# Routing from raw rows and one pipeline of 80 expert tiles: a change to the end of a conv-attention and mixture-of-experts block

## The chip, the cores and the metric

The kernel runs on one core of a Trainium2 chip. The metric is the device time of one execution in microseconds, as the median of a few runs. A profile of one execution comes with it; its time is given beside its span.

## The reference

The input is `x` of 8 x 32 x 32 x 192 in float32, that is 8192 tokens of 192 channels. Two attention layers with 12 heads come first; this case leaves both as they are. What matters here is the last part:

```python
x = x + conv_attention(group_norm(x))
t = tokens(x)
t = t + attention(layer_norm(t))          # the residual that routing starts from
t = t + experts(layer_norm(t))

def experts(t):                           # 16 experts, 192 -> 192 -> 192
    idx = argmax(t @ Wg.T + bg)           # one expert for each token
    for e in range(16):
        h = gelu(t @ W1[e].T + b1[e])
        out += (idx == e) * (h @ W2[e].T + b2[e])
```

The layer norm in front of the experts takes a mean and a variance over the 192 channels of each token, and has no weights: `(v - mean) / sqrt(var + 1e-5)`.

## The kernel before

The program is a row of stages, each a block of its own in which the five engines run their own lists of instructions and meet only at semaphores. Between two blocks all engines meet. The stages are: projections, attention with relative positions, projections, attention (`a2`), routing (`r`), experts (`e`). Only the last three matter here.

**Attention, `a2`.** It runs in 24 steps of 16 blocks, two steps to an iteration. SP's list holds stores of results, the rows of maxima that PE waits for at the start of a step, and work for later stages, held by the class `Early`: the residual rows (`early.tokens`, one DMA in each iteration but the first) and the experts' weights (`early.weights`).

**Routing, `route`.** 8192 tokens go in 4 rounds of 2048, a round being 16 tiles of 128 tokens (NT = 16). In a round:

- SP loads the attention outputs of the round in 6 DMAs (`load_attn`, L1178) into one of two buffers. `load_attn(0)` is the first thing in its list; the two small loads of the gate's weights and bias (L1182, L1183) follow, and `load_attn(1)`.
- DVE (`normalise`) adds them to the residual (L1307), takes the moments of each token (L1311, L1315), writes the mean behind the row (L1318), and hands variance + eps (L1319) to POOL, which raises it to -1/2 (`root`, L1219). DVE waits for that and writes normalised rows to a buffer of their own (L1323, 16 instructions).
- SP stores the residual rows with mean and root behind them to DRAM (`X3`, L1193); the experts read them from there.
- PE transposes the normalised rows (L1255), ACT copies them from PSUM (L1289), and PE multiplies them with the gate's weights (L1262, 64 passes of 16 columns).
- DVE (`choose`) adds the bias (L1336), finds the first largest logit (L1339 to L1344) and, with two products of PE (L1267, L1270, the ranks), the place of each token in its expert's list. Each step waits for the one before through the semaphore `ch`.
- POOL (`list_tokens`, L1224) writes the token numbers to their places with 16 scatters, each of 128 numbers of 4 bytes, to DRAM (`SLOTS`).

DVE's order is normalise(0), then for each round normalise(r + 1) and choose(r). PE's order is, for each round, transposes, logits, ranks. POOL issues the root of round r + 2 between the halves of the list of round r. After the last round DVE works out from the counts which expert each of 80 tiles belongs to and where its slots stand. POOL waits until all 64 scatters have landed and loads the slots (L1239).

**Experts, `experts`.** 80 tiles of 128 slots, in a hardware loop of two passes over 40 unrolled tiles (UN = 40). POOL gathers the rows of a tile from `X3` (L1476) into one of NB = 8 buffers and scatters results to the output (L1464). The scatter of tile k - LAG follows the gather of tile k, with LAG = NB - 2 = 6. DVE normalises (L1568); PE transposes (psX), applies layer one (psH), transposes again (psG) and applies layer two (psY), each one tile behind the other; ACT copies and applies gelu (L1536, L1548); DVE adds the residual (L1574). PE reads the tile's expert number from SBUF into a register. At the end of a pass POOL waits for all scatters; the next pass starts empty. POOL clears all gather buffers once before the first gather (L1458).

Of the kernel before, what the change touches and what calls it, by code (L numbers as in the profile page):

```python
# [42 lines left out]
def attention(nc, name, rel, scale, QK, RL, RLH, VN, OD, onehot_dram, early=None):  # L43
# [13 lines left out]
    with ExitStack() as ctx:  # L57
# [205 lines left out]
        def _(sp):  # L263
# [48 lines left out]
            def step(i, u, jobs, base, first, last):  # L312
# [770 lines left out]
def route(nc, name, XR, xl, X2DONE, ON, WG, BG, X3, SLOTS, TR, IXA):  # L1083
# [7 lines left out]
    with ExitStack() as ctx:  # L1091
# [9 lines left out]
        Os = [sb(f"attn{i}", [P, 2, NG, KT, GH * HD]) for i in range(2)]  # L1101
        XMs = [sb(f"xm{i}", [P, NT, C]) for i in range(2)]
        XT = sb("xmT", [CC, 2, PAIR])
# [5 lines left out]
        BGs = sb("bg", [P, E_N])  # L1109
        LG = sb("logits", [P, NT, E_N])  # L1110
# [31 lines left out]
        psL = ps("psL", [P, 512])  # L1142
# [6 lines left out]
        oload = [sem(f"oload{i}") for i in range(2)]  # L1149
# [14 lines left out]
        CH = 13 + NPRE  # L1164
        NM = 5
# [8 lines left out]
        def _(sp):  # L1174
# [6 lines left out]
            load_attn(0)  # L1181
# [16 lines left out]
        def _(pool):  # L1198
# [44 lines left out]
        def _(pe):  # L1243
            pe.wait_ge(made, NMADE)
            pe.wait_ge(wload, 32)
            for r in range(ROUNDS):
                XM = XMs[r % 2]
                pe.wait_ge(nm, r * NM + 5)
                for t in range(NT):
# [3 lines left out]
                    for c in range(2):  # L1253
                        at = 2 * P * (t % 2) + P * c
                        mm = nc.tensor.transpose(psT[0:CC, t // 2 % 4, at:at + P], XM[:, t, CC * c:CC * c + CC],  # L1255
                                                 ident[:, :])
                    if t % 2 == 1:
                        mm.then_inc(xtp, 1)
                pe.wait_ge(xts, r * (NT // 2) + NT // 2)
                for t in range(NT):  # L1260
                    for c in range(2):
                        mm = nc.tensor.matmul(psL[:, E_N * t:E_N * t + E_N], XT[:, c, P * t:P * t + P], WGs[:, c, :],  # L1262
                                              start=(c == 0), stop=(c == 1))
                mm.then_inc(lg, 1)

                pe.wait_ge(ch, r * CH + 6)
                nc.tensor.matmul(psK[:, 0:NT * E_N], TRI[:, :], OH[:, :, :].rearrange("p t e -> p (t e)"),  # L1267
                                 start=True, stop=False)
                pe.wait_ge(ch, r * CH + (8 + NPRE))
# [25 lines left out]
        def _(dve):  # L1295
            dve.wait_ge(wload, 32)
            dve.wait_ge(made, NMADE)
            dve.wait_ge(xl, X2DONE)
            nc.vector.tensor_copy(IDI[:, :], IDF[:, :]).then_inc(ids, 1)

            def normalise(r):
                X, XM, at = XR[:, tiles(r), :], XMs[r % 2], r * NM
# [14 lines left out]
                dve.wait_ge(nm, at + 2)  # L1317
                nc.vector.tensor_copy(X[:, :, C:C + 1], MV[:, :, 0:1]).then_inc(nm, 1)  # L1318
                nc.vector.tensor_scalar(VE[:, :, :], MV[:, :, 1:2], EPS, None, ALU.add).then_inc(nm, 1)  # L1319
                dve.wait_ge(nm, at + 4)  # L1320
# [4 lines left out]
                ins.then_inc(nm, 1)  # L1325

            def choose(r):
                n = [0]

                def link(ins):  # L1330
# [3 lines left out]

                dve.wait_ge(lg, r + 1)
                link(nc.vector.tensor_tensor(LG[:, :, :], psL[:, 0:NT * E_N].rearrange("p (t e) -> p t e", e=E_N),  # L1336
                                             BGs[:, :].rearrange("p (o e) -> p o e", o=1).to_broadcast([P, NT, E_N]),
                                             ALU.add))
# [60 lines left out]
def experts(nc, name, X3, W, wl, WDONE, TLs, IXA, OUT):  # L1399
# [4 lines left out]
    UN = 40  # L1404
    NB = 8
    LAG = NB - 2
    assert NTILE == 2 * UN and UN % NB == 0
    with ExitStack() as ctx:
# [42 lines left out]
        def _(pool):  # L1451
# [15 lines left out]
            with pool.Fori(0, NTILE // UN) as i:  # L1467
# [19 lines left out]
        def _(pe):  # L1487
# [15 lines left out]
            with pe.Fori(0, NTILE // UN) as i:  # L1503
# [25 lines left out]
        def _(act):  # L1529
# [8 lines left out]
            with act.Fori(0, NTILE // UN) as i:  # L1538
# [17 lines left out]
        def _(dve):  # L1556
# [4 lines left out]
            with dve.Fori(0, NTILE // UN) as i:  # L1561
# [16 lines left out]
class Early:  # L1578
# [6 lines left out]
    def __init__(self, nc, ctx, X2, weights):  # L1585
        self.X = ctx.enter_context(nc.sbuf_tensor("f_x", [P, T // P, CM], F32))
        self.W = [ctx.enter_context(nc.sbuf_tensor(f"f_w{i}", [CC + 1, 2, E_N, C], F32)) for i in (1, 2)]
        self.xl = ctx.enter_context(nc.semaphore("f_xl"))
        self.wl = ctx.enter_context(nc.semaphore("f_wl"))
# [14 lines left out]
def hybrid_block(nc, a, out):  # L1604
# [21 lines left out]
    with ExitStack() as ctx:  # L1626
# [4 lines left out]
        route(nc, "r", early.X, early.xl, early.XDONE, O2, a["wg"], a["bg"], X3, SLOTS, TR, IXA)  # L1631
# [53 lines left out]
```

## Time and profile before

| | us |
|---|---|
| median of 3 runs | 3399.32 |
| lowest and highest run | 3392.03, 3401.49 |
| the profiled execution | 3392.6 |
| its span | 3391.0 |
| mean granted TensorE clock | 0.896 of full speed |
| routing, from the block's start to the last wait for scatters | 2926 to 3108 |
| experts, from the first gather to the end | 3119 to 3391 |

The difference between the profiled time and the span lies ahead of the first and behind the last recorded instruction. In the rows below a line of the timeline gives the start and the duration in microseconds, the engine, the line of the kernel, the operation, what it writes and reads, the count, and in square brackets how long the engine had been idle before it and what ended that. A row of the groups gives busy time and mean ns of one instruction, then the idle time before these instructions and what ended it. A row of the windows gives the stretch, its length, for PE, PEld (weight loads), DVE, ACT and POOL the busy time and the count, and then the granted clock as a share of full speed, the busy share of the DMA engines, and GB/s.

### The profile page before, as it was taken

What the parts mean: (1) busy time and instruction counts of PE and PEld (TensorE: products, weight loads), DVE (VectorE), ACT (ScalarE), POOL (GpSimd) and SP (SyncE); (2) the same over time, 40 slices, a digit from 0 to 9 for tenths busy, and PEclk for the clock granted to TensorE, in tenths of its full rate; (3) what the DMA queues carried; (4) which work ended last, traced back from release to release, by engine and by line L of the source; (5) the groups of instructions that cost most, each with busy time, mean ns of one, the idle gap of its engine ahead of it and who ended that gap; (6) DMA issues with size and microseconds to landing.
All of it is one profiled execution on the core that took longest, in us unless ns stands there. A gap on an engine that the chain in (4) does not pass through costs nothing. (4 is left out here: it accounts for less than half of the span.)

```text
span 3391.0 us, 64293 instructions
## 1 busy us (share of the span) xinstructions
PE 2932.4 (86%) x17814; PEld 1145.2 (34%) x17815; DVE 2457.8 (72%) x4481; ACT 1852.6 (55%) x2382; POOL 1034.4 (31%) x1685
## 2 busy tenths in 40 slices
PE   4887699999999999996995999999999999662877
PEld 2665122222222222224652222222222222261666
DVE  3553698998899998943645999999999999351211
ACT  1343066776666666672331577777777777410332
POOL 0000333333333333313222223333333332154655
PEclk9777599999999999997986899999999999865777
DMA  4766555444554445524655432222222222360211
GB/s 80 206 199 196 116 105 105 103 100 96 100 109 101 95 98 101 108 54 115 179 165 118 90 89 74 74 74 72 74 73 74 75 72 59 114 54 11 58 50 34
DMA packets 234003, 327.80 MB, mean 97 GB/s; under 512 B 63820, under 2 KB 162966, under 8 KB 229298
## 3 DMA queue, kind: packets, MB, share of 16 engines
q0 software_dynamic: 76576, 192.17, 25.7%
q1 hardware_dynamic: 157332, 134.44, 15.5%
q8 instruction: 51, 0.84, 0.1%
q14 instruction: 44, 0.36, 0.1%
HBM read 217.71 MB, written 109.19 MB: 96 GB/s over the span
## 5 line engine op out<-in xcount | busy, mean ns | idle before, releaser
L499 DVE TENSOR_REDUCE a_halfmax<-a_psR 128x1 f32<-128x512 f32 x3072 | 1964.0, 685 | 193.0 <-PE a_psR L350 174.7
L454 ACT ACTIVATE a_probs<-a_psS 128x1024 f32<-128x1024 f32 x1536 | 1488.4, 1021 | 795.2 <-PE a_psS L368 790.8
L368 PE MATMUL a_psS<-a_qrows,a_krows 121*128 121x512 f16 (+1 forms) x3072 | 807.7, 385 | 53.6 <-DMA a_qrows<-relh 49.2
L379 PE MATMUL a_psO<-a_probs,a_v 128*32 128x512 f32 x6144 | 827.9, 611 | 1.2 <-ACT a_probs L454 1.2
L350 PE MATMUL a_psR<-a_kmax,a_qmax 64*128 64x512 f16 x3072 | 685.4, 400 | 80.2 <-DMA a_qmax<-relh 43.3
L350 PEld LDWEIGHTS a_psR<-a_kmax,a_qmax 64*128 64x128 f16 x3072 | 161.1, 93 | 1072.2 <-DVE a_halfmax L499 951.5
L368 PEld LDWEIGHTS a_psS<-a_qrows,a_krows 121*128 121x128 f16 (+1 forms) x3072 | 243.2, 98 | 427.9 <-issue 163.1
L204 POOL DMA_DIRECT2D a_qmax<-qk x240 | 122.4, 510 | 666.8 <-PE a_psO L379 601.6
L188 POOL DMA_DIRECT2D a_qrows<-qk x240 | 123.6, 515 | 276.6 <-PE a_psO L379 257.2
L830 PE MATMUL p_psQ<-p_xnT,p_wqk 96*128 96x512 f32 x384 | 190.3, 660 | 20.4 <-DVE p_xnT L987 13.9
L379 PEld LDWEIGHTS a_psO<-a_probs,a_v 128*32 128x32 f32 x6144 | 121.4, 108 | 184.2 <-issue 175.9
L1574 DVE TENSOR_TENSOR e_y<-e_psY,e_x 128x192 f32<-128x192 f32 x80 | 28.6, 357 | 173.8 <-PE e_psY L1499 103.5
L1021 DVE SCALAR_TENSOR_TENSOR p_half<-p_qk,p_sc,p_half 128x2048 f16<-128x2048 f32 (+1 forms) x36 | 72.8, 2031 | 110.8 <-ACT p_half L925 110.8
L918 ACT ACTIVATE p_qk<-p_psQ,p_bqk 128x512 f32<-128x512 f32 x96 | 65.6, 686 | 144.3 <-PE p_psQ L830 144.3
L205 POOL DMA_DIRECT2D a_kmax<-qk x240 | 121.9, 508 | 15.8
L830 PEld LDWEIGHTS p_psQ<-p_xnT,p_wqk 96*128 96x128 f32 x384 | 80.2, 213 | 126.5 <-issue 111.9
L193 POOL DMA_DIRECT2D a_qrows<-rel x96 | 48.4, 504 | 209.7 <-PE a_psO L379 208.3
L200 POOL DMA_DIRECT2D a_v<-v x96 | 53.5, 557 | 190.8 <-PE a_psO L379 190.1
L873 PE MATMUL p_psR<-p_half,p_relThalf 64*128 64x64 f16 x1920 | 97.5, 239 | 14.8 <-DVE p_rel L1059 12.7
L933 ACT CAST p_rel<-p_psR 128x256 f16<-128x256 f32 x192 | 57.2, 391 | 92.2 <-PE p_psR L873 92.2
L1499 PE MATMUL e_psH<-f_w,e_xmT 96*128 (+1 forms) x320 | 89.8, 415 | 16.1 <-ACT e_xmT L1536 9.5
L1464 POOL DMA_INDIRECT out<-e_y,e_slots x80 | 81.0, 1013 | 73.9 <-DVE e_y L1574 49.5
(162 smaller groups left out, 2310.8 us busy)
## 6 DMA issues: line engine op xcount, KB each, us to landing
a_qrows<-qk POOLq DMA_DIRECT2D x240, 128.0 KB, 4.0
qk<-p_half SPq DMA_DIRECT2D x96, 256.0 KB, 3.4
v<-p_v SPq DMA_DIRECT2D x48, 512.0 KB, 6.2
a_qrows<-rel POOLq DMA_DIRECT2D x96, 256.0 KB, 4.6
a_v<-v POOLq DMA_DIRECT2D x96, 256.0 KB, 3.1
a_krows<-qk POOLq DMA_DIRECT2D x168, 128.0 KB, 3.8
a_qmax<-qk POOLq DMA_DIRECT2D x288, 64.0 KB, 2.3
a_kmax<-qk POOLq DMA_DIRECT2D x240, 64.0 KB, 2.3
```

The lines of the kernel that those rows point to most:

```text
L188: pool.dma_start(A[buf][c][at, :, :], qk(s, TERMS[n][0], 0)).then_inc(loaded[buf], 16)
L204: pool.dma_start(AM[buf][0][of, :, :], qk_pair(s, TERMS[n][0], 0, r)).then_inc(loadedm[buf], 16)
L205: pool.dma_start(KM[buf][of, :, :], qk_pair(s, TERMS[n][1], 1, r)).then_inc(loadedm[buf], 16)
L350: mm = nc.tensor.matmul(psR[:, slot, :], AM[b][half][at, p, P * qt:P * qt + P], KM[b][at, p, 512 * half:512 * half + 512], start=True, sto ...
L368: mm = nc.tensor.matmul(psS[:, (2 * n + j) % 4, :], K[buf][:, h, keys], A[buf][kt % NA][:, h, queries], start=True, stop=True)
L379: mm = nc.tensor.matmul(psO[32 * h:32 * h + 32, :], V[buf][:, kt, h, :], PT[:, blk % 2, h, :], start=(kt == 0), stop=(kt == KT - 1))
L454: nc.scalar.activation(PT[:, blk % 2, 2 * pair:2 * pair + 2, :], psS[:, b0:b0 + 2, :], ACT.Exp, scale=scale).then_inc(exped, 1)
L499: nc.vector.tensor_reduce(mx[:, unit, half:half + 1], psR[:, slot, :], AX.X, ALU.max)\
L830: mm = nc.tensor.matmul(psQ[:, n % 2, :], WQK[:, c, P * m:P * m + P], XN[:, c, 512 * q:512 * q + 512], start=(c == 0), stop=(c == 1))
L873: mm = nc.tensor.matmul(o[:, :, x, :], table.rearrange("p k h -> p (k h)"), q[:, :, xx, :] if hw == 0 else q[:, :, :, xx], start=(i == 0), ...
L1464: pool.indirect_dma_start(OUT, bass.IndirectOffsetOnAxis(ap=IX[:, k:k + 1], axis=0), Y[:, q, :], None, bounds_check=T - 1, oob_is_err=Fals ...
L1499: mm = nc.tensor.matmul(dst[:, 0:C], xT[0:k, c, :], w[0:k, c, bass.ds(e, 1), :] .rearrange("p o n -> p (o n)"), start=(c == 0), stop=(c == 1))
```

## The change

In attention's last iteration SP loads the attention outputs of routing's first round, one DMA a block, in six blocks, after it has waited that the earlier steps' stores are done. In routing PE works on the raw residual rows instead of normalised ones. By `(x - m) r W = r (x W - m sum(W))` the mean and the root are applied to the 16 logits: DVE multiplies the mean with the column sums of the gate's weights (two small products of PE), subtracts, multiplies with the root, and adds the bias. Normalised rows are no longer written. PE's logits run one round ahead of its ranks, with a second PSUM bank; DVE's moments run two rounds ahead of its choice, and POOL's roots three ahead. The experts become one unrolled pipeline of 80 tiles with ten buffers, the scatter eight tiles behind the gather.

```diff
@@ attention, SP
+                    if early is not None and last and u == 0 and blk == 6:
+                        for qh in range(QH):
+                            sp.wait_ge(stored[qh], 16 + 16 * 2 * NG)
+                    if early is not None and last and u == 0 and blk in range(6, 12):
+                        sp.wait_ge(pvdone, s * PVS + blk + 2)
+                        early.attn(sp, OD, blk - 6)
@@ class Early
+        self.O = ctx.enter_context(nc.sbuf_tensor("f_attn", [P, 2, NG, KT, GH * HD], F32))
+    def attn(self, sp, OD, n):
+        sp.dma_start(self.O[:, n // NG, n % NG, :, :], OD[n]).then_inc(self.ol, 16)
@@ route, SP
-            load_attn(0)
             sp.dma_start(WGs[:], ...)
@@ route, POOL
             root(0)
             root(1)
+            root(2)
...
-                if r + 2 < ROUNDS:
-                    root(r + 2)
+                if r + 3 < ROUNDS:
+                    root(r + 3)
@@ route, PE
-                pe.wait_ge(nm, r * NM + 5)
+            for c in range(2):
+                mm = nc.tensor.matmul(psC[:, 0:E_N], ONE[0:CC, :], WGs[:, c, :], start=(c == 0), stop=(c == 1))
+            mm.then_inc(wsum, 1)
+            def logits(r):
+                pe.wait_ge(x3, r + 1)
...
+            logits(0)
+            for r in range(ROUNDS):
+                if r + 1 < ROUNDS:
+                    logits(r + 1)
+                ranks(r)
@@ route, DVE
-            dve.wait_ge(wload, 32)
...
-                dve.wait_ge(rsq, r + 1)
-                for t in range(NT):
-                    ins = nc.vector.tensor_scalar(XM[:, t, :], X[:, t, 0:C], X[:, t, C:C + 1], X[:, t, C + 1:C + 2],
-                                                  ALU.subtract, ALU.mult)
...
+                link(nc.vector.tensor_tensor(MS[:, :, :], X[:, :, C:C + 1].to_broadcast(wide),
+                                             WS[:, :].rearrange("p (o e) -> p o e", o=1).to_broadcast(wide), ALU.mult))
                 dve.wait_ge(lg, r + 1)
+                link(nc.vector.tensor_tensor(LG[:, :, :], psL[:, r % 2, 0:NT * E_N]..., MS[:, :, :], ALU.subtract))
+                dve.wait_ge(rsq, r + 1)
+                link(nc.vector.tensor_tensor(LG[:, :, :], LG[:, :, :], X[:, :, C + 1:C + 2].to_broadcast(wide), ALU.mult))
+                link(nc.vector.tensor_tensor(LG[:, :, :], LG[:, :, :], BGs[:, :]..., ALU.add))
...
             normalise(0)
+            dve.wait_ge(wload, 32)
+            dve.wait_ge(wsum, 1)
+            nc.vector.tensor_copy(WS[:, :], psC[:, 0:E_N]).then_inc(wsum, 1)
+            normalise(1)
+            dve.wait_ge(wsum, 2)
             for r in range(ROUNDS):
-                if r + 1 < ROUNDS:
-                    normalise(r + 1)
+                if r + 2 < ROUNDS:
+                    normalise(r + 2)
                 choose(r)
@@ experts
-    UN = 40
-    NB = 8
+    UN = NTILE
+    NB = 10
     LAG = NB - 2
...
-            with pool.Fori(0, NTILE // UN) as i:
+            for i in range(1):
```

## Rows read from the trace of the kernel before

**Rows 1.** The page, busy time and share of the span by engine

```profile
PE 2932.4 (86%) x17814; PEld 1145.2 (34%) x17815; DVE 2457.8 (72%) x4481; ACT 1852.6 (55%) x2382; POOL 1034.4 (31%) x1685
```

**Rows 2.** Timeline of routing, single instructions

```profile
2930.26 1.01 POOL L1214 MEMSET r_empty<- 128x1104 int32 x1
...
2935.45 0.20 DVE L1299 CAST r_tokenIdsInt<-r_tokenIds 128x64 int32<-128x64 f32 x1 [9.70 <-DMA r_bg<-in_bg]
...
2977.82 0.17 DVE L1359 CAST r_placeOfInt<-r_placeOf 128x16 int32<-128x16 f32 x1
...
2978.89 1.87 POOL L1224 DMA_INDIRECT slots<-r_tokenIdsInt,r_placeOfInt  x1 [14.09 <-DVE r_placeOfInt L1359]
...
3041.62 11.03 PE L1262 MATMUL r_psL<-r_wg,r_xmT 96*128 96x16 f32 x63 [1.28 <-ACT r_xmT L1289]
...
3060.50 0.42 DVE L1336 TENSOR_TENSOR r_logits<-r_psL,r_bg 128x256 f32<-128x256 f32 x1 [23.24 <-remote]
...
3068.93 0.95 POOL L1224 DMA_INDIRECT slots<-r_tokenIdsInt,r_placeOfInt  x1 [11.49 <-DVE r_placeOfInt L1359]
...
3087.85 0.96 POOL L1224 DMA_INDIRECT slots<-r_tokenIdsInt,r_placeOfInt  x1 [0.30 <-issue]
...
3107.64 0.94 POOL L1239 DMA_INDIRECT r_slotsOfTile<-slots,r_slotRow  x1 [18.83 <-DMA slots<-r_tokenIdsInt,r_placeOfInt]
...
3110.72 0.22 DVE L1394 CAST r_slotsOfTileF<-r_slotsOfTile 80x128 f32<-80x128 int32 x1 [37.22 <-DMA r_slotsOfTile<-slots,r_slotRow]
```

**Rows 3.** Groups by line in routing, 2926 to 3112 us

```profile
L1224 POOL DMA_INDIRECT slots<-r_tokenIdsInt,r_placeOfInt x64 | 64.5, 1008 | 53.5 <-DVE r_placeOfInt L1359 35.5 <-issue 18.0
...
L1262 PE MATMUL r_psL<-r_wg,r_xmT 96*128 96x16 f32 x256 | 42.5, 316 | 8.4 <-ACT r_xmT L1289 4.7 <-issue 3.5
...
L1255 PE MATMUL r_psT<-r_ident,r_xm 128*96 128x128 f32 x128 | 20.9, 341 | 27.8 <-DVE r_xm L1323 27.8
...
L1323 DVE TENSOR_SCALAR r_xm<-f_x 128x192 f32<-128x192 f32 x64 | 19.9, 389 | 16.3 <-POOL f_x L1219 16.3
...
L1311 DVE BATCH_NORM_STATS2 r_stats<-f_x 128x6 f32<-128x192 f32 x64 | 17.0, 345 | 0.1
...
L1307 DVE TENSOR_TENSOR f_x<-f_x,r_attn 128x1536 f32<-128x1536 f32 x8 | 13.7, 1754 | 0.1
...
L1315 DVE BATCH_NORM_AGGREGATE r_meanvar<-r_stats 128x2 f32<-128x6 f32 x64 | 4.7, 151 | 0.1
...
L1219 POOL TENSOR_TENSOR f_x<-r_variance,r_half 128x16 f32<-128x16 f32 x4 | 11.8, 2944 | 27.7 <-DVE r_variance L1319 27.7
```

**Rows 4.** Windows of two stretches, the wait for scatters and the experts

```profile
3076.00:3116.00 40.00, 0.40 (x1) 0.18 (x1) 0.47 (x2) 0.00 (x0) 12.22 (x16) 0.50 0.01 1
...
3254.00:3300.00 46.00, 36.27 (x174) 30.51 (x174) 10.07 (x30) 17.30 (x47) 27.15 (x27) 0.79 0.20 55
```

**Rows 5.** Groups by line in the experts, 3110 to 3391 us

```profile
L1499 PE MATMUL e_psH<-f_w,e_xmT 96*128 (+1 forms) x320 | 89.8, 415 | 16.1 <-ACT e_xmT L1536 9.5 <-issue 6.0 <-ACT e_h L1548 0.6
...
L1464 POOL DMA_INDIRECT out<-e_y,e_slots x80 | 81.0, 1013 | 73.9 <-DVE e_y L1574 49.5 <-issue 19.3 <-DMA out<-e_y,e_slots 5.1
...
L1493 PE MATMUL e_psX<-e_ident,e_xm 128*96 128x128 f32 x160 | 39.3, 336 | 32.3 <-DVE e_xm L1568 30.1 <-issue 2.1
...
L1458 POOL MEMSET e_x<- 128x1552 f32 x1 | 1.4, 1396 | 0.1
```

**Rows 6.** Timeline of POOL in the experts: scatters of tiles 4, 30, 43, 47, 73

```profile
3145.34 1.02 POOL L1464 DMA_INDIRECT out<-e_y,e_slots  x1 [2.49 <-DVE e_y L1574]
...
3227.38 1.02 POOL L1464 DMA_INDIRECT out<-e_y,e_slots  x1 [2.50 <-DVE e_y L1574]
...
3274.89 1.02 POOL L1464 DMA_INDIRECT out<-e_y,e_slots  x1 [2.20 <-DVE e_y L1574]
...
3287.66 1.02 POOL L1464 DMA_INDIRECT out<-e_y,e_slots  x1 [2.51 <-DVE e_y L1574]
...
3371.82 1.02 POOL L1464 DMA_INDIRECT out<-e_y,e_slots  x1 [2.04 <-DVE e_y L1574]
```

More of the change, by code:

```diff
@@ L1080, with route @@
 EMPTY = 1 << 20
[L1083 removed]
+def route(nc, name, early, ON, WG, BG, X3, SLOTS, TR, IXA):
     NT = PAIR // P
@@ L1099, in sem @@
             return ctx.enter_context(nc.semaphore(f"{name}_{n}"))
-        Os = [sb(f"attn{i}", [P, 2, NG, KT, GH * HD]) for i in range(2)]
-        XMs = [sb(f"xm{i}", [P, NT, C]) for i in range(2)]
-        XT = sb("xmT", [CC, 2, PAIR])
+        XR = early.X
+        Os = [early.O, sb("attn", [P, 2, NG, KT, GH * HD])]
+        XT = sb("xT", [CC, 2, PAIR])
         ST = sb("stats", [P, NT, 6])
@@ L1109, in route @@
         BGs = sb("bg", [P, E_N])
+        WS = sb("wgSums", [P, E_N])
+        MS = sb("meanPart", [P, NT, E_N])
         LG = sb("logits", [P, NT, E_N])
@@ L1141, in route @@
         psT = ps("psT", [P, 4, 512])
-        psL = ps("psL", [P, 512])
+        psL = ps("psL", [P, 2, 512])
         psK = ps("psK", [P, 512])
@@ L1148, in route @@
         filled = sem("filled")
-        oload = [sem(f"oload{i}") for i in range(2)]
+        oload = [early.ol, sem("oload")]
+        wsum = sem("wsum")
         x3 = sem("x3")
@@ L1163, in route @@
         NPRE = NT.bit_length() - 1
-        CH = 13 + NPRE
-        NM = 5
+        CH = 16 + NPRE
+        NM = 4
         NMADE = 12
@@ L1245, in _ @@
             pe.wait_ge(wload, 32)
-            for r in range(ROUNDS):
-                XM = XMs[r % 2]
-                pe.wait_ge(nm, r * NM + 5)
+            for c in range(2):
[3 more added lines that the diff above has]
+                pe.wait_ge(x3, r + 1)
                 for t in range(NT):
@@ L1259, in _, with ranks @@
                 pe.wait_ge(xts, r * (NT // 2) + NT // 2)
+                if r >= 2:
+                    pe.wait_ge(ch, (r - 2) * CH + 2)
                 for t in range(NT):
                     for c in range(2):
-                        mm = nc.tensor.matmul(psL[:, E_N * t:E_N * t + E_N], XT[:, c, P * t:P * t + P], WGs[:, c, :],
+                        mm = nc.tensor.matmul(psL[:, r % 2, E_N * t:E_N * t + E_N], XT[:, c, P * t:P * t + P], WGs[:, c, :],
                                               start=(c == 0), stop=(c == 1))
                 mm.then_inc(lg, 1)
-                pe.wait_ge(ch, r * CH + 6)
+            def ranks(r):
+                pe.wait_ge(ch, r * CH + 9)
                 nc.tensor.matmul(psK[:, 0:NT * E_N], TRI[:, :], OH[:, :, :].rearrange("p t e -> p (t e)"),
                                  start=True, stop=False)
-                pe.wait_ge(ch, r * CH + (8 + NPRE))
+                pe.wait_ge(ch, r * CH + (11 + NPRE))
                 nc.tensor.matmul(psK[:, 0:NT * E_N], ONE[:, :], PRE[NPRE % 2][:, :, :].rearrange("p t e -> p (t e)"),
                                  start=False, stop=True).then_inc(rk, 1)
+            logits(0)
[3 more added lines that the diff above has]
+                ranks(r)
             pe.wait_ge(ch, ROUNDS * CH)
@@ L1295, in _ @@
         def _(dve):
-            dve.wait_ge(wload, 32)
             dve.wait_ge(made, NMADE)
-            dve.wait_ge(xl, X2DONE)
+            dve.wait_ge(early.xl, early.XDONE)
             nc.vector.tensor_copy(IDI[:, :], IDF[:, :]).then_inc(ids, 1)
             def normalise(r):
-                X, XM, at = XR[:, tiles(r), :], XMs[r % 2], r * NM
+                X, at = XR[:, tiles(r), :], r * NM
                 dve.wait_ge(oload[r % 2], r // 2 * 96 + 96)
@@ L1399, in experts @@
 def experts(nc, name, X3, W, wl, WDONE, TLs, IXA, OUT):
-    UN = 40
-    NB = 8
+    UN = NTILE
+    NB = 10
     LAG = NB - 2
-    assert NTILE == 2 * UN and UN % NB == 0
+    assert UN % NB == 0
     with ExitStack() as ctx:
@@ L1501, in layer @@
                 mm.then_inc(done, 1)
-            with pe.Fori(0, NTILE // UN) as i:
+            for i in range(1):
                 ex = [None] * UN
@@ L1536, in to_sbuf @@
                 nc.scalar.copy(dst[0:CC], src[0:CC, 0:2 * P].rearrange("p (c t) -> p c t", c=2)).then_inc(done, 1)
-            with act.Fori(0, NTILE // UN) as i:
+            for i in range(1):
                 n = i * UN
@@ L1560, in _ @@
             nc.vector.sem_inc(ys, 2)
-            with dve.Fori(0, NTILE // UN) as i:
+            for i in range(1):
                 n = i * UN
@@ L1587, in __init__ @@
         self.W = [ctx.enter_context(nc.sbuf_tensor(f"f_w{i}", [CC + 1, 2, E_N, C], F32)) for i in (1, 2)]
+        self.O = ctx.enter_context(nc.sbuf_tensor("f_attn", [P, 2, NG, KT, GH * HD], F32))
         self.xl = ctx.enter_context(nc.semaphore("f_xl"))
+        self.ol = ctx.enter_context(nc.semaphore("f_ol"))
         self.wl = ctx.enter_context(nc.semaphore("f_wl"))
```

17 lines of the change are left out of this document (10 added, 7 removed).

## The prediction

> **What bounds the kernel now.** The page comes first. PE is busy for 86% of the span [rows 1], but the change touches only the end: the routing of tokens to experts (from about 2926 us) and the expert layers (3118 to 3391 us). Of attention it touches only what SP issues in the last steps. So I went on to the windows by stage, the groups by line, and the instructions in order of time, of these 465 us.
>
> In routing no engine is the bound for long. DVE starts only when two small loads have landed, 9.70 us after it was free [rows 2]. From then on the four rounds are a chain: DVE adds and takes moments, POOL takes the root, DVE normalises (64 instructions, 19.9 us, after 16.3 us of waiting for POOL), PE transposes and multiplies, DVE chooses [rows 3]. The last round shows the cost: DVE sits idle for 23.24 us before it can read the logits at 3060.50 [rows 2]. POOL's 64 scatters of token numbers take 64.5 us, with 0.3 us between two, and wait 35.5 us for places [rows 3]. But POOL is not the last word: its last 16 scatters are issued from 3068.93 on, the last one at 3087.85, and it then waits 18.83 us, until 3107.64, until they have landed [rows 2]. In those 40 us nothing else is busy, and the DMA share is 0.01 [rows 4]. I read that as scatters that land more slowly than they are issued. That share can't show where writes are pending; the wait can.
>
> In the experts PE looks like the bound (four groups of matmuls: psH 89.8, psX 39.3 us, and two like them [rows 5]), but at a granted clock of 0.79 [rows 4], so between its levels of 1.2 and 2.4 GHz, which it falls between when it waits. POOL issues a gather and a scatter for each tile: 2 x (1.01 + 0.30) = 2.64 us. Its scatters 4 and 30 start 82.0 us apart, 43 and 73 start 96.9 us apart [rows 6]: 3.16 and 3.23 us a tile. The pattern repeats every 12.8 us (3274.89, 3287.66): four tiles are 10.6 us of issue and about 2.2 us of waiting for a result [rows 6].
>
> **Routing, the issuing side.** (a) The first attention outputs are loaded during attention's last steps, and the two small loads go first and are awaited only after the first moments. DVE can start when POOL's constants stand, at 2930.26 + 1.01 = 2931.3, instead of 2935.45 [rows 2]: 4.2 us. The six loads that move onto SP in attention are about 0.4 us of queue time each, behind waits for values that PE has long been past; behind them in the queue stands only the store of the half step, whose data is not read until its own load. I cost this at nothing; if the row of maxima after them came late, PE would wait, at most some 3 us, once.
> (b) The normalisation goes: 19.9 us of DVE and the 16.3 us in front of it. Three operations on 256 elements a round (scaled mean, times root, plus bias) come in, 0.42 us each by the operation that reads the logits now [rows 2] and 0.04 between them: 1.4 us a round. One round before the choice is now (13.7 + 17.0 + 4.7)/4 = 8.9, with the two small copies 9.3 us [rows 3].
> (c) DVE does three of these before its first choice: 2931.5 + 27.9 + 0.2 = 2959.6. PE starts its first round at about 2935 and needs (20.9 + 42.5)/4 = 15.9, with the turn through ACT 17 us a round [rows 3]. It does two rounds before the first ranks: 2969. The ranks' second product and the four last operations add about 4 us, and POOL starts 0.9 us later, as before (2977.82 + 0.17 to 2978.89 [rows 2]): 2974 against 2978.9, so 4.9 us earlier. Here the round ahead costs something: without it the first list would start at about 2970.
> (d) After that POOL is the slowest of the issuing side: 16 x 1.31 = 21 us a round against 17 + 2.4 for PE and 9.3 + 9.2 for DVE (20 steps of at most 0.46), and one root of 2.9 us among them [rows 3]. Its last scatter would be out at 2974 + 84 + 3 = 3061, before at 3087.85 + 0.96 = 3088.8 [rows 2]: 28 us earlier.
>
> **Routing, the landing side.** The slots can be read only when all 64 have landed. No row gives a scatter's landing, so its price is bounded. I take 3 us for the first to land, as the load of the slots behind them took (3107.64 to 3110.72 [rows 2]). All 64 then took 3107.6 - 2981.9 = 125.7 us, or 1.96 us each, with gaps and with two of the stores of the residual between them. The last 16 alone took 3107.6 - 3071.9 = 35.7 us, or 2.23 us each [rows 2]. Both are more than the 1.31 us of an issue. If the landing rate is what counts, an earlier issue only lengthens the queue. At 1.96 the end moves by what the start moves: -4.9 us (3102.7). At 2.23 it is 2977 + 142.7 = 3119.7: +12 us. I take 1.96, because the changed stage too has stores among its scatters; 2.23 stays in the range. The other end is a landing that keeps up with the issue: 3061 plus the 18.8 us tail of before, -28 us, or at the most 3061 + 3, -44 us. PE's logits of the last round took 18.9 us (3041.62 to 3060.50 [rows 2]) where the mean is 10.6 [rows 3]; if all rounds are so slow, PE sets 27 us a round and the last list starts some 14 us later than POOL alone would have it, still before the landing at 3102.7.
>
> The Trainium skill ("DMA: Bandwidth & Descriptors", Anatomy of one DMA) says that a DMA has about 2 us of fixed cost, mostly the receipt of the write, after which the semaphore fires. By that rule alone every scatter would be in 2 us after its issue: the first rival at its far end. The wait of 18.83 us behind the last issue [rows 2] speaks against it. The same page (Specifications) says that writes below 512 B are done as a read and a write; the scatters write 4 B each, and this agrees with a rate below that of the issue.
>
> **Experts.** (e) One pipeline of 80 in place of two of 40. Scatters 30 and 43 are 3274.9 - 3227.4 = 47.5 us apart; at 3.2 us a tile it would be 41.6 [rows 6]. So the drain and refill cost 5.9 us, and they go.
> (f) Ten buffers, and a scatter that follows its gather by eight tiles. If POOL's wait goes away, a tile costs 2.64: -0.56 x 70 = -39 us. If it stays, nothing. PE's weight: its matmul groups fill most of the stage, it waited only 32.3 us before psX, much of that at the two starts [rows 5], and a POOL that has scattered all finished tiles must wait whatever its buffers. More buffers let PE find a fifth tile in a period now and then: (10.6 + 2.2)/4 = 3.2 becomes 13.2 + 2.2 over 5 = 3.08. I take -0.1 x 70 = -7 us, near the end at zero, because the wait of 2.2 us is for results, not for buffers.
> (g) The clearing of the gather buffers grows by a quarter (1.4 us [rows 5]) on the way to the first gather: +0.4. Constants in place of register sums shorten queues that the rows show as hidden: nothing. If code for the second 40 tiles has to be fetched and that were late, it would cost some us; the first 40 had the same need and ran at 3.16, no slower than the second.
>
> **Sum**: -4.9 - 5.9 - 7 + 0.4 = -17.4. The profiled execution took 3392.6 us (span 3391.0), which is 6.7 below the median of the three runs. 3392.6 - 17.4 = 3375.2, and beside the median 3382.
>
> **Rivals.**
> - The landing keeps up with the issue: -28 instead of -4.9, total -40, 3359 (-56 and 3343 if it trails by 3 us alone). For it: the stores that shared the DMA engines are earlier too. Against: 2.23 us each for the last 16, with nothing beside them. The Trainium skill's fixed cost (above) would have it so. 0.17.
> - Ten buffers free POOL: 2.64 us a tile, total -49, 3350. For it: 49.5 us of POOL's waits were for results [rows 5], some of which start from late gathers. Against: PE's own groups. A fuller PE would also keep its clock. 0.13.
> - Nothing but the drain goes, and landing costs 2.23: +12.2 - 5.9 + 0.4 = +6.7 at no gain a tile, -0.3 with it; 3399 to 3406, no change that can be told. 0.22.
> - The other side: with scatters queued without a break the landing gets slower, not only longer. It decides from 64 x (R - 1.96) = 17.4 + 10, R = 2.39 us; at 2.5 it is +17, 3416. For it: 2.23 beats 1.96 where less else ran. 0.18.
> - My forecast: 0.30, between 3374 and 3390.
>
> The bound of a change that can be told is 0.3% or 10 us here. Faster: the first two, the forecast: 0.60; same 0.22; slower 0.18. Both signs hold chances, so 8 in 10 need 3350 (the second rival) to 3410 (between +6.7 and +17); the forecast's own range is 3370 to 3392.
>
> **What would show it.** POOL's first scatter at about 2974 and its last before 3065; then a wait of some 40 us for landing until about 3103, against 18 before: that is the step I lean on. If the wait is under 25 us and ends before 3085, the first rival holds; beyond 3125, the fourth. DVE's long wait for the last logits is gone. In the experts no gap in the middle, and 3.1 us a tile; at 2.7 the second rival holds. PE's clock there stays near 0.8. The prediction is wrong at its root if the landing time isn't a rate per scatter.

## The result and the profile after

The changed kernel takes 3358.48 us (median of 4, 3352.58 to 3363.97) beside 3395.68 us for the kernel before (4 runs, 3388.42 to 3401.49): a ratio of 0.9888, 95% interval 0.9865 to 0.9911, or 38 us less (30 to 46). I had forecast 17.4 us less, 3375 to 3382 us. The time lies in the wide range (3350 to 3410), which was drawn to take in rivals on both sides, but below the forecast's own (3370 to 3392); the gain is more than twice what I summed.

The profiled execution spans 3350.9 us, 40.1 less than before's. The first thing to read is where the touched stages begin. Timeline, attention's last output, of before and then of the changed kernel:

```profile
2925.33 0.42 DVE L519 TENSOR_TENSOR a_out<-a_psR,a_recip 128x256 f32<-128x256 f32 x1
```

```profile
2909.25 0.42 DVE L525 TENSOR_TENSOR a_out<-a_psR,a_recip 128x256 f32<-128x256 f32 x1
```

16.1 of the 40.1 us had been gained by then, in stages whose code is the same but for six late loads. All of it is there before the second attention begins (its first loads: 1831.8 and 1815.7 us). So from here on I count from attention's last output; the experiments show that this offset is chance. Behind it stand 465.7 us before and 441.7 after: 24.0 less, 16.6 of them up to the first gather (193.6 and 177.0), 7.4 behind it (272.0 and 264.7).

Timeline of routing in the changed kernel, the rows that answer to [rows 2]:

```profile
2915.25 0.20 DVE L1319 CAST r_tokenIdsInt<-r_tokenIds 128x64 int32<-128x64 f32 x1 [5.58 <-POOL r_empty L1222]
...
2957.14 0.42 DVE L1378 TENSOR_TENSOR r_place<-r_psK,r_expertBase 128x256 f32<-128x256 f32 x1 [7.53 <-PE r_psK L1285]
...
2959.60 1.86 POOL L1232 DMA_INDIRECT slots<-r_tokenIdsInt,r_placeOfInt  x1 [13.60 <-DVE r_placeOfInt L1382]
...
2963.44 10.15 PE L1276 MATMUL r_psL<-r_wg,r_xT 96*128 96x16 f32 x64 [1.06 <-ACT r_xT L1310]
...
2989.01 0.60 PE L1276 MATMUL r_psL<-r_wg,r_xT 96*128 96x16 f32 x2 [1.02 <-issue]
...
2998.18 0.19 PE L1276 MATMUL r_psL<-r_wg,r_xT 96*128 96x16 f32 x1 [2.61 <-issue]
...
3013.46 0.42 DVE L1378 TENSOR_TENSOR r_place<-r_psK,r_expertBase 128x256 f32<-128x256 f32 x1 [28.85 <-PE r_psK L1285]
...
3015.28 1.02 POOL L1232 DMA_INDIRECT slots<-r_tokenIdsInt,r_placeOfInt  x1 [10.78 <-DVE r_placeOfInt L1382]
...
3054.70 0.96 POOL L1232 DMA_INDIRECT slots<-r_tokenIdsInt,r_placeOfInt  x1 [0.30 <-issue]
...
3074.78 0.95 POOL L1248 DMA_INDIRECT r_slotsOfTile<-slots,r_slotRow  x1 [19.12 <-DMA slots<-r_tokenIdsInt,r_placeOfInt]
```

Read it from the end. The wait for landing is 19.12 us, as long as before's 18.83 [rows 2], although the last 32 scatters now follow each other without a break; my forecast needed some 40 us here. So the slots are read when the issuing side is done plus 19 us. The issuing side in turn has one hole, 10.78 us, and the rows above it say whose: DVE waits 28.85 us for ranks that stand in PE's queue behind the last round's logits, and after the first 36 of them those come one or two at a time, mostly with 0.5 to 2.6 us of "issue" ahead of each. The round before, at 2963.44, was not held up, though POOL had been issuing scatters since 2959.60. Windows over these stretches (busy us and instructions of PE, PEld, DVE, ACT, POOL; granted clock, DMA share, GB/s) show PE all but empty in the second stretch while POOL issues, and at the lower of its levels (0.50, 1.2 GHz):

```profile
2975.00:2987.00 12.00, 10.34 (x69) 9.66 (x69) 7.75 (x24) 4.84 (x16) 9.09 (x10) 0.78 1.17 81
2987.00:3009.00 22.00, 4.34 (x21) 5.07 (x20) 0.00 (x0) 0.00 (x0) 13.40 (x14) 0.50 0.47 28
...
3150.00:3200.00 50.00, 38.75 (x191) 33.97 (x190) 9.65 (x30) 14.63 (x45) 31.59 (x31) 0.81 0.20 56
```

Groups by line in the experts, changed kernel (against [rows 5]): matmuls (psH 88.0 us) and scatters as before, and POOL's waits for results 40.6 us where they were 49.5.

```profile
L1492 POOL DMA_INDIRECT out<-e_y,e_slots x80 | 81.3, 1016 | 66.8 <-DVE e_y L1602 40.6 <-issue 21.8 <-DMA out<-e_y,e_slots 4.3
```

### The profile page after: what moved, and what is told of

It reads as the page before. It is cut to its first block and busy times, and to the rows that moved or that the text cites. A ratio compares the mean times of both kernels' runs of the same rounds, so it can differ in the third digit from the quotient of the medians.

```text
span 3350.9 us, 63879 instructions
## 1 busy us (share of the span) xinstructions
PE 2924.0 (87%) x17818; PEld 1147.6 (34%) x17818; DVE 2438.7 (73%) x4430; ACT 1849.2 (55%) x2379; POOL 1037.2 (31%) x1684
## 5 line engine op out<-in xcount | busy, mean ns | idle before, releaser
L836 PE MATMUL p_psQ<-p_xnT,p_wqk 96*128 96x512 f32 x384 | 188.5, 654 | 19.3 <-DVE p_xnT L993 13.9
L1564 ACT COPY e_xmT<-e_psX 96x256 f32<-96x256 f32 x80 | 29.5, 369 | 196.9 <-PE e_psX L1521 179.1
L1492 POOL DMA_INDIRECT out<-e_y,e_slots x80 | 81.3, 1016 | 66.8 <-DVE e_y L1602 40.6
```

Source lines behind the costliest of these rows:

```text
L836: mm = nc.tensor.matmul(psQ[:, n % 2, :], WQK[:, c, P * m:P * m + P], XN[:, c, 512 * q:512 * q + 512], start=(c == 0), stop=(c == 1))
L1492: pool.indirect_dma_start(OUT, bass.IndirectOffsetOnAxis(ap=IX[:, k:k + 1], axis=0), Y[:, q, :], None, bounds_check=T - 1, oob_is_err=Fals ...
```

## The experiments

One table first, worked out from each kernel's timeline: attention's last output (us from the span's start), and from there POOL's first scatter, the end of its last, the load of the slots, the first gather; then first gather to end, and the time between results 35 and 45 of the experts.

```
kernel                    attention  first  last   slots  gather  to end  35-45
before                      2925.3   53.6  163.5  182.3  193.6   272.0   40.4
changed                     2909.3   50.4  146.4  165.5  177.0   264.7   30.0
e1 route only               2913.0   47.8  140.4  158.5  169.8   274.2   39.1
e2 experts only             2909.6   56.9  179.8  199.0  210.5   258.6   31.2
e3 eight buffers            2924.3   50.4  143.8  161.8  173.0   262.3   30.5
e4 no round ahead           2924.0   44.0  159.2  176.7  188.2   261.1   32.6
e5 no scatters of results   2922.4   50.4  141.4  157.3  168.8   163.0   17.5
e6 56 scatters              2920.7   47.9  130.8  142.2  153.0   261.4   30.6
e7 22 scatters              2917.4   47.8  114.4  130.2  139.1   259.8   30.4
e8 known expert             2914.0   50.4  144.2  159.9  171.3   253.6   27.0
e9 results nowhere          2929.3   47.8  143.3  159.4  171.0   265.5   33.9
e10 gathers nowhere         2928.5   50.3  143.8  160.0  171.7   266.1   29.6
e11 late loads              2913.0   51.2  159.6  175.1  186.6   262.4   30.7
e12 set up early            2912.9   50.4  143.0  159.8  167.3   263.5   31.3
```

The first column runs from 2909.3 to 2929.3 with no tie to the kernel: before, e2 and e11, which have no early loads, have 2925.3, 2909.6 and 2913.0; e3, e9 and e10, which have them, 2924.3 to 2929.3. So the 16.1 us of the first comparison are no effect of the change that these profiles show.

A second thing varies between profiles, in routing. Take, in each kernel, the time from a round's first transpose on PE to its last logit. In twelve of the fourteen kernels one round is held up, while all others take 16.8 to 19.7 us: 35.9 us in the changed kernel, 40.6 in e2, 31.8 in e4 (its third round), 20.7 in e5, 48.3 in e11, 30.9 to 35.0 in the other seven. Before's slowest took 19.4 and e7's 17.3. So before's 193.6 us to the first gather were a good draw: e2, with the same routing, has 210.5.

**e1 and e2: the change in two halves.** e1 has the changed routing and loads with before's experts, e2 the reverse.

```diff
-    UN = NTILE
-    NB = 10
+    UN = 40
+    NB = 8
```

> The changed routing and early loads with the experts of before (two turns of 40 tiles, eight buffers). In the profiled execution of the changed kernel the stretch from attention's last output to the first gather is 177.0 us, before it is 193.6: 16.6 us less. Theory A (the gain of the whole change is what the touched stages show, 16.6 in routing and 7.4 in the experts): this kernel gains about 17 us on the kernel before, ratio 0.995, its first gather comes about 177 us after attention's last output, and first gather to end is about 272 us, as before. Rival (the other 16 us, which the profile shows in stages whose code is the same, belong to the change, by way of the early loads or where things lie in memory): it gains 30 us or more, and its attention ends about 16 us earlier than before's. Rival of the prediction (the experts gain more than they show alone): under 10 us.

> The kernel before with the experts alone changed: one run of 80 tiles, ten buffers. Theory A: first gather to end is about 265 us instead of 272, the gain is 7 us, ratio 0.998, all of it the drain in the middle. Prediction's step (f), 0.1 us a tile from the buffers: 12 to 13 us, ratio 0.996. Rival (changed stages shift others by where code and data lie): more than 15 us, with attention's end moved.

e1: 0.9931 (0.9907 to 0.9955), 23 us (15 to 32) less. e2: 0.9959 (0.9941 to 0.9977), 14 us (8 to 20) less. Together 37, the whole, so nothing suggests that the halves touch each other. e1's interval allows theory A's 17 us and just reaches the rival's 30; e1's attention did end 12.3 us earlier than before's, but e2's, without the early loads, ended 15.7 us earlier. In e2, POOL stood 27.15 us before its last list, where before's stood 11.49 [rows 2].

**e3: eight buffers.**

```diff
-    NB = 10
+    NB = 8
```

> The changed kernel with eight buffers instead of ten, still one run of 80 tiles. Theory A (what a tile costs does not hang on buffers): the time of the changed kernel within 2 us, 3.2 us a tile, about 37 us under the kernel before. Rival (the ten buffers do give 0.1 us a tile and something else takes it back): 7 us slower than the changed kernel, 3.3 us a tile.

0.9905 (0.9880 to 0.9930), which overlaps the changed kernel's interval; the time alone doesn't exclude 7 us. The tiles do: results 5 to 35 and 45 to 75 come every 3.16 us (mean of both) with eight buffers, every 3.15 with ten (changed, e2, e4, e11: 3.10 to 3.21). A gain of 0.1 us a tile from the last two buffers is not there; one of a few hundredths couldn't be told with one profile of e3.

**e4: no round ahead.**

```diff
-            logits(0)
             for r in range(ROUNDS):
-                if r + 1 < ROUNDS:
-                    logits(r + 1)
+                logits(r)
                 ranks(r)
```

> The changed kernel, but PE makes the ranks of a round before the logits of the next one (no round ahead). In the changed kernel DVE waits 7.53 us for the first ranks behind the second round's logits, and POOL's first scatter is 50.4 us after attention's last output. Theory A: the first scatter comes 7 to 8 us earlier, POOL is the slowest of the issuing side, and the last scatter is out 5 to 8 us earlier, so 5 to 8 us under the changed kernel. Rival (PE's logits of the last rounds are what POOL waits for, 10.78 us in the changed kernel, and without the round ahead each such slow round is paid in full): the last scatter is out 5 to 15 us later, and the kernel is slower by as much.

0.9947 (0.9929 to 0.9964), 14 us worse than e3 on the same chip. Both expectations were half right: the first scatter is 6 us earlier than in the changed kernel and e3 (44.0 against 50.4; 4 us against the kernels with 47.8), but POOL then waits 18.36 and 12.29 us for the third and fourth list, and the last scatter is out 13 to 19 us later. The round ahead costs at the start and pays at the end.

**e6 and e7: fewer scatters of token numbers.** e6 leaves out the last 8, e7 all but the first of each half list in the first three rounds. The slots not written stay empty, so some rows aren't gathered. Each has one run, its profile.

```diff
-                list_tokens(r, NT // 2, NT)
+                if r < ROUNDS - 1:
+                    list_tokens(r, NT // 2, NT)
```

```diff
-                for t in range(t0, t1):
+                for t in range(t0, t1 if r == ROUNDS - 1 else t0 + 1):
```

> The changed kernel; left out are the last 8 of the 64 scatters of token numbers, so that the list of the last 1024 tokens stays empty. POOL's wait for landing behind its last issue was 17.5 to 19.3 us in six profiles. Theory R (a rate: about 2.2 us a scatter at the end, 1.26 to issue): the wait gets shorter by 8 x (2.2 - 1.26) = 8 us, to about 11, and the slots are read 18 us earlier. Theory D (a delay: a scatter takes some 19 us to land however many are behind it): the wait stays at 18 to 19 us, the slots are read 10 us earlier.

> The changed kernel; left out are 14 of the 16 scatters of each of the first three rounds, so that 6 are issued there and the 16 of the last round follow alone. Theory A (PE's logits of round 3, 25 to 30 us where an undisturbed round takes 10, are held up by the scatters in flight): they take 10 to 13 us, and PE's waits for its own issue between them (9.5 to 16.9 us) are gone. Rival (the stores of the residual hold them up): they stay above 18 us. For landing, theory R (rate): the last 16 need 3 + 16 x 2.2 = 38 us from the first issue, a wait of 18 us behind the last; theory Q (a backlog of all 64): under 8 us; theory D (delay): 18 to 19 us.

POOL's load of the slots in e6, and in e7:

```profile
3062.95 0.95 POOL L1249 DMA_INDIRECT r_slotsOfTile<-slots,r_slotRow  x1 [11.39 <-DMA slots<-r_tokenIdsInt,r_placeOfInt]
```

```profile
3047.58 0.95 POOL L1248 DMA_INDIRECT r_slotsOfTile<-slots,r_slotRow  x1 [15.86 <-DMA slots<-r_tokenIdsInt,r_placeOfInt]
```

With 8 fewer the wait falls to 11.39 us, as theory R had it; a fixed delay of 19 us is out. e7, with the last 16 alone, waits 15.86, near theory R's 18 and not under 8: the first three rounds leave hardly any backlog. Yet a single rate would leave a longer wait behind 24 scatters without a break (e6) than behind 16 (e7), and it was shorter. Over an unbroken run, less 3 us for the first, a scatter lands in 1.6 us (e6, 24 of them), 1.65 to 1.77 (32 of them, the nine kernels with the changed order) or 2.05 to 2.26 (16 of them: before, e2, e4, e7). The wait depends on how many went last, but one number a scatter doesn't give it; what else sets it is open.

e7 answers the second question too. Its logits of the last round on PE's timeline:

```profile
2987.84 10.56 PE L1276 MATMUL r_psL<-r_wg,r_xT 96*128 96x16 f32 x64 [1.17 <-ACT r_xT L1310]
```

All 64 run on in 10.56 us; in the changed kernel the same 64 take 29.5 us (2981.95 to 3011.5), and in the others with all scatters and this order 13.7 (e5) to 26.6. The stores of the residual run in both, so they alone don't hold PE up; the scatters are needed. They are not enough: the round before took 10.15 us beside them, and e4's last round 10.1. In the changed kernel the last residual store was issued at 2973.89, just ahead of the round that is held up; scatters without stores weren't tried.

**e5, e9, e10: which part of POOL's work the experts feel.** e5 leaves out the scatters of results for tiles 0 to 69, and with them the gathers' waits for those scatters. e9 issues those with row numbers out of bounds, so that nothing is written; e10 does that to all gathers and writes all results, computed from zeros. The diffs are e5's, and the one of e9 and e10.

```diff
+                if k >= UN - NB:
                     pool.indirect_dma_start(OUT, bass.IndirectOffsetOnAxis(ap=IX[:, k:k + 1], axis=0), Y[:, q, :], None,
```

```diff
-  bass.IndirectOffsetOnAxis(ap=IX[:, k:k + 1], axis=0)
+  bass.IndirectOffsetOnAxis(ap=NO[:, 0:1], axis=0)
```

> The changed kernel; left out are the scatters of the experts' results for tiles 0 to 69 (only the last ten are written), so POOL issues one indirect DMA a tile, a gather, instead of two: 1.31 us instead of 2.62. A tile costs 3.10 to 3.19 us in the kernels with one run of 80 tiles. Theory A (POOL's two issues and the waits round them set the tile, as in the prediction's terms): the tile falls to PE's own work, about 2.5 us (36.27 us of 46 in a window of before, at a granted clock of 0.79, rows 4, x 3.2), the kernel gains 40 us or more on the changed one. Theory B (PE's matmuls and the way they are released set it, whatever POOL does): 3.1 us, no change beyond 5 us. Theory C (PE's results come late while POOL issues, so the lateness goes with the issues but part of the chain stays): in between, 2.7 to 2.9 us.

> The changed kernel; the scatters of results of tiles 0 to 69 are issued as before, but with row numbers out of bounds, so POOL spends its 1.3 us on each and nothing is written (those rows of the output stay unwritten). Without those issues a tile costs 1.78 us, with them and their writes 3.10 to 3.19. Theory I (the time of POOL's issues, 2 x 1.31 = 2.62 us, is the bound, and the rest is how PE meets it): 2.6 to 2.75 us a tile, about 30 us less than the changed kernel. Theory W (the writes that the scatters set off hold PE's results or POOL's waits back): under 2.6 us is impossible by the issues, so 2.62 with PE at its high clock as well; the two differ in the next run. Theory P (PE's results come late whenever POOL issues two a tile, written or not): 3.1 us, no change.

> The changed kernel; the scatters of results are real, but all gathers have row numbers out of bounds, so POOL spends the same time on them and nothing is read (PE works on zeros, the output is wrong). Theory P (what two issues a tile do to PE, whatever moves): 3.1 us a tile. Theory W (the scatters' writes are what delays): 3.0 to 3.1 us a tile here too, but 2.6 where the scatters go nowhere. Theory G (the landing of gathers, some 9 us ahead of their use, sets the pace): 2.6 to 2.75 us here.

e5: 0.9614 (0.9595 to 0.9632), some 93 us under the changed kernel, 1.78 us a tile, below even theory A. e9: 0.9906 (0.9877 to 0.9934); e10: 0.9900 (0.9880 to 0.9919): no gain, 3.14 and 3.22 us a tile. Windows of the same stretch, e5, then e9:

```profile
3150.00:3200.00 50.00, 50.00 (x345) 47.88 (x344) 18.37 (x57) 27.49 (x87) 28.10 (x30) 1.00 0.19 50
```

```profile
3150.00:3200.00 50.00, 40.00 (x188) 34.85 (x186) 9.40 (x29) 14.51 (x44) 32.69 (x32) 0.76 0.11 28
```

With one issue a tile PE is never idle and runs at its upper level (1.00, 2.4 GHz). With two, though the DMA share falls from 0.20 to 0.11, it is back between its levels. The 50 us hide that it is at one level or the other. Two neighbouring stretches of e9:

```profile
3187.90:3194.70 6.80, 5.84 (x20) 5.01 (x21) 1.85 (x6) 2.38 (x8) 4.24 (x5) 0.50 0.08 20
3194.70:3201.50 6.80, 4.17 (x28) 3.54 (x27) 1.29 (x4) 2.06 (x7) 3.93 (x4) 1.00 0.17 43
```

In the changed kernel, between its 6th and 79th gather, PE spends 109 us at the lower level, 92% busy, with 3.1 matmuls started a us, and 123 us at the upper, 71% busy, with 4.3; in e5 at the upper level it starts 6.8. A tile has 12 matmuls. By an estimate from these numbers a tile takes 3.9 us at the lower level, 2.8 at the upper, and 1.75 where PE is never short of work. So at the lower level PE, nearly full, can't keep up with POOL's 2.62 us; at the upper it can, and its busy share is near 1.78/2.62 = 0.68.

The timeline of e5 and of e9 shows the two rhythms:

```profile
3201.63 1.00 POOL L1503 DMA_INDIRECT e_x<-x,e_slots  x1 [0.75 <-issue]
```

```profile
3198.52 1.03 POOL L1507 DMA_INDIRECT e_x<-x,e_slots  x1 [0.30 <-issue]
3199.30 0.33 ACT L1579 ACTIVATE e_h<-e_psH 128x192 f32<-128x192 f32 x1 [3.11 <-PE e_psH L1530]
3199.69 0.42 PE L1524 MATMUL e_psG<-e_ident,e_h 128*96 128x128 f32 x2 [1.50 <-issue]
3200.81 0.36 DVE L1605 TENSOR_TENSOR e_y<-e_psY,e_x 128x192 f32<-128x192 f32 x1 [4.56 <-remote]
...
3202.08 1.02 POOL L1495 DMA_INDIRECT out<-e_y,e_nowhere  x1 [2.54 <-DVE e_y L1605]
```

POOL issues back to back (0.30 between two) until it has no result left. Meanwhile psH, whose matmuls are recorded at 3197.38 to 3198.19, is read only at 3199.30; the result of the tile is late in turn, and POOL waits 2.54 us for it, whether it writes that result or not. Theory P's number holds against those of W and G: with two issues a tile it stays at 3.1 to 3.2 us whatever moves, and 2.62 of it is the issues themselves. What makes up the rest isn't settled. The clock is a rival that the expectations didn't name: POOL's pace leaves PE idle, the lower level follows, and there PE is slower than POOL.

**e8: no reading of the expert.**

```diff
-                        ex[m] = pe.value_load(TLs[0:1, bass.ds(n + m, 1)], min_val=0, max_val=E_N - 1)
+                        ex[m] = m // (UN // E_N)
```

> The changed kernel; PE takes the expert of a tile as a constant (tile number / 5) instead of reading it from the routing's list, so results of most tiles are computed with another expert's weights, and the read and the register sums of addresses go. Theory A (PE's instruction stream, its loads and address sums, is what makes its results late): the tile falls below 3.0 us, 10 us or more in all. Theory B (they are hidden): 3.1 us, no change beyond 3 us.

The profile has 253.6 us to the end and 3.06 us a tile, the fastest of those with all issues, but the ratio is 0.9884 (0.9863 to 0.9905), the changed kernel's. Undecided: a gain over the changed kernel is not shown.

**e11: the loads back in routing.**

```diff
+            load_attn(0)
             sp.dma_start(WGs[:], WG.rearrange("(c p) n -> p c n", p=CC)).then_inc(wload, 16)
```

> The changed kernel, but the first round's attention outputs are loaded in the routing block again, ahead of the two small loads (part (a) of the change undone). In the changed kernel DVE starts its additions 6.1 us after attention's last output, before 10.2 us. By the prediction's step (a): DVE starts 4.2 us later, and the first scatter comes 4 us later, at 52 to 54 us behind attention's last output where six runs had 47.8 or 50.4. Rival (PE or POOL have slack that takes it up): DVE's start moves, the first scatter does not.

DVE's additions start 9.9 us behind attention instead of 6.1, the first scatter at 51.2 where others had 47.8 or 50.4. So the start moves by step (a)'s 4 us and the first scatter by 1 to 3. The third list then came 24 us behind the second: PE's transposes of the last round, begun at 2980.1, were still followed by a wait of 19.17 us ahead of its logits at 3014.5. Whether the loads did that or chance, one profile can't say.

**e12: POOL's setting up inside the wait.** From its trace of the changed kernel: after the slots are read, POOL clears and copies for 5 us before the first gather. Here it does so while the last scatters land.

```diff
             pool.wait_ge(scat, ROUNDS * 16 * NT)
```
(ahead of this line now stand the identity, the rows of ones and the clearing of `e_x`; the gathers read `f_slotsAll` itself)

> The changed kernel; what POOL does at the start of the experts' block (identity, rows of ones, clearing of ten gather buffers: 3.7 us to the first gather's list, in the changed kernel's trace 3081.34 to 3084.99) is done in the routing block, in POOL's wait for the last scatters to land (15.5 to 19.3 us in eleven profiles), and the slots are used where they stand instead of being copied (1.26 us). Theory A (that wait is dead time for POOL): from the slots' load to the first gather 11.1 to 11.6 us become 6.5 us, 5 us less in all, with the landing wait shorter by what POOL does in it and the slots read as early as before. Rival (landing goes on more slowly while POOL works, or other engines' block change takes the time anyway): the first gather comes less than 2 us earlier. The time goes to about 33 + 5 us under the kernel before, ratio 0.989.

Slots' load to first gather: 7.5 us, in the changed kernel 11.5. The slots are read no later (159.8 us; 157.3 to 165.5 in the others with this routing, but for e11). That is 4 of the 5 us. The time, 3355.79 us and 0.9899 (0.9878 to 0.9921), can't be told from the changed kernel's. Of the kernels that compute everything, none is shown to be faster than the changed one.

## Why the prediction was right or wrong

**(a) Right.** DVE starts 6.0 us behind attention's last output, 10.1 before: 4.1, forecast 4.2. What reaches the first scatter is less (e11).

**(b), (c) Right.** A round before the choice takes 9.1 us (9.3 forecast); the four operations on the logits take 0.42 each. The first scatter moved by 3.2 us (4.9 forecast), and its price for the round ahead is there as I said: 7.53 us of DVE waiting, and 4 to 6 us in e4 where I had said 4.

**(d), issuing side: the bound failed, and the size in part.** I had POOL as the slowest, at 21 us a round, and DVE's long wait for logits gone. PE's last round took 35.9 us instead of 17 (2975.5 to 3011.5), DVE waited 28.85 us for the ranks behind it, and POOL 10.78 before the third list. Forecast 28 us earlier than before; measured 17.1, and 19 to 23 in seven more profiles of this routing (all but e11's), against before's one good draw. By place the forecast was nearer: 135.7 us behind attention's last output, measured 140.4 to 146.4. I had seen one slow round in before (18.9 us from its first logit to DVE's reading, 13.1 of them recorded matmuls) and priced it as harmless because landing would be later anyway; landing wasn't.

**(d), landing: this step failed, and it is the bulk of the error.** I divided the time from the first scatter to the read of the slots by 64 and called the 1.96 us a landing rate. But of the 128.7 us from the first scatter to the reading, POOL's issuing took 109.9 (2978.9 to 3088.8), with 21.4 us of waiting for lists among them (the 35.5 us of [rows 3], less 14.09 ahead of the first scatter). The quotient was the pace of issuing. Landing comes to some 1.6 to 1.8 us a scatter over long runs, has hardly any backlog after POOL's pauses (e7), and ends 15.5 to 19.3 us behind the last issue in every profile but e6's. So what moves the last issue moves the end. This term was -4.9; the first gather moved by 16.6 in the two first profiles, and by 30 between the means: 193.6 and 210.5 for the old routing, 168.8 to 177.0 (seven profiles, mean 171.8) for the new. Two profiles make a weak mean; e1's time says 23 (15 to 32). The first rival, with a chance of 0.17, had the mechanism, a kept tail of 18.8, and its own sign came in (a wait under 25 us that ends before 3085: 19.12, 3074.78); it put the last issue too early. Its total, 3359, is nearer the measured time than the forecast's.

By the Trainium skill ("DMA: Bandwidth & Descriptors", Anatomy of one DMA), every scatter would be in about 2 us after its issue. The direction that this gave, an end that moves with the last issue, was right. The number was not: the wait was 15.5 us and more, and 11.4 with 8 fewer.

**(e) Right in kind, too small.** The drain was 5.9 us in my sum; results 35 to 45 take 40.4 and 39.1 us with two turns, 30.0 to 32.6 without (changed, e2, e3, e4, e11; mean 31.0): 8.8.

**(f) Failed as a mechanism.** Ten buffers give nothing that e3 can tell. The mean tile away from the middle fell from 3.19 (before, e1) to 3.15, some 3 us in all, no more than it differs between profiles. My reason, that PE would find a fifth tile now and then, supposed that PE's time was its own; e5, e9 and e10 show that it depends on how many DMAs POOL issues a tile. (2 x 1.31 is 2.62 us, not 2.64; this changes nothing.) Drain and tiles together: -12.9 forecast, -11.3 between the means (273.1 and 261.8). That sum was right by luck, two errors that nearly cancel.

**(g) Right**: clearing takes 1.72 us, 0.3 more.

So the gain was too small through the landing term, by 12 us in the first pair, 18 by e1's time and 25 between the means. That the time still fell in the wide range is owed to the rivals' bounds, not to the mechanism I leaned on. The second rival, POOL alone at 2.64 us a tile, did not come: no kernel with two issues a tile averaged below 3.06.

**Open.** By which path POOL's issues slow PE. In routing the clock can't be all of it: single matmuls of 0.19 us have up to 2.6 us of "issue" ahead of them. Fetching of PE's code is a rival there, but only two packets of it, 0.86 and 2.68 us long, are recorded near the 29.5 us. In the experts the clock could make up most of it, by the estimate above, but no run kept the clock up with two issues a tile. What the rows show is PE without instructions ("issue") or with results later than the recorded end. The Trainium skill ("Perfetto Trace Analysis", Tensor Engine Instruction) says that the profiler estimates a matmul's end; the trace agrees, with consumers up to 1.1 us late in the rows shown, and that is one reason why the recorded busy time can't settle it. A kernel with both gathers and scatters going nowhere, and one with a short pause behind each issue, weren't tried. Nor did e5 separate fewer issues from longer pauses between them.

## What to carry to other kernels

Before a quotient of a stretch is used as a rate, take out the time in which the feeding side stood still; and to price an unseen landing, remove a few of the last transfers and look at the wait. If a kernel is issued by POOL's indirect DMAs, count the issues a tile first: leaving out nearly half of them gave 93 us here (with most results unwritten, so it is a price and not a gain to be had), two more buffers nothing that could be told. Read the clock by short stretches and not as a mean. Measure a change from the last mark that it can't move, and take a second profile of the kernel before: 16 of the first 40 us were not the change's own, and before's routing differed by 17 us between two profiles.

## What the runs showed of the hardware

PE's supply can suffer from POOL's back-to-back indirect DMAs: in one round of routing 64 small matmuls took 10.56 us with most of the scatters left out and 13.7 to 29.5 us with all of them in the same order, while other rounds ran beside scatters in 10.1 us. In the experts a tile takes 3.14 and 3.22 us with two issues, one kind of which moves nothing, and 1.78 with one issue; the granted clock goes with it (0.76 in e9, 1.00 in e5). Runs of indirect scatters of 128 times 4 B are in after 1.6 to 2.3 us each (less 3 us for the first), where one takes 1.26 us to issue. And nearly the same code up to the end of attention took 2909.3 to 2929.3 us over 14 profiles.
